# First routing of a mixture-of-experts layer: picks for all 32 tiles at once, expert starts added by TensorE, one-hots built tile by tile

## The chip, the cores and the metric

The kernel runs on one core of one Trainium2 chip. The metric is the device time of one execution in microseconds (us), as the median of several runs. The five engines are TensorE (PE; its weight loads are PEld), VectorE (DVE), ScalarE (ACT), GpSimd (POOL) and SyncE (SP), which issues most transfers.

## The reference

4096 rows of 128 values pass three layers, each with its own layer norm and a residual:

```python
x = x + 0.5 * ffn(layernorm(x))
x = x + attention(layernorm(x), context)
x = x + 0.5 * ffn(layernorm(x))

def ffn(x):                                   # 8 experts, 128 -> 512 -> 128
    gate_logits = einsum('bsd,ed->bse', x, gate_w) + gate_b + expert_bias
    top_idx = argmax(gate_logits, axis=-1)
    for e in range(8):
        mask = (top_idx == e)[..., None]
        h = relu(einsum('bsd,df->bsf', x, w1[e]) + b1[e])
        out = out + mask * (einsum('bsf,fd->bsd', h, w2[e]) + b2[e])
```

Only the expert with the largest logit serves a row. The attention has 8 heads of 128 and 512 keys from `context`; its scores are sharpened around their mean, and its bias `bout` is added at the end.

## The kernel before, in words

The 4096 rows lie in SBUF as 128 partitions x 32 tiles (`ROWS`, T = 32, two halves of HALF = 16 tiles, four chunks of CH = 8). A row is served by its expert in a sorted order: the rows of each expert fill whole tiles of 128 *slots*, at most SLOTS = 39 tiles. The kernel has three parts: the first expert layer with its routing and the preparation of the attention weights, the attention in 256 units with the second routing beside them, and the second expert layer. Each engine runs its own program, written out by hand; semaphores order them, and an engine that waits holds back everything behind it in its program.

The change is in the first 40 us, the first routing. In the order of the kernel's steps:

- `x_stats`, `x_moments` and `x_shift_of` (VectorE) and a power on GpSimd (L523) make the layer norm's scale and shift of each chunk. `x_transposes` and `x_gate` (TensorE) make the logits, half the tiles in bank 2, half in bank 3. `store_stats` (SP) writes each chunk's rows out to `x_stats` once its shift is there.
- `pick_rows(hf)` (VectorE, L899) turns the logits of one half into one-hots over the experts, `OHA`, in seven dependent steps, and sums them over the tiles (`SUMS`).
- `ranks0(hf)` (TensorE, L1441) counts for each row how many rows of the same expert stand before it: one matmul with `BEFORE`, 15 with `ONES`, and for the second half one for the sums of the first. `totals0` (L1457) counts the rows of each expert.
- `split_ranks(hf)` (VectorE, L927) picks the rank of the row's own expert and splits it into rank modulo 128 (`LOF`) and the rest (`HIF`). `places` (L984) works out from the totals how many tiles each expert has and where its slots start, picks that start for each row (L992, L994) and adds the rest of the rank over 128 (L995): the slot tile of each row, `SIDX`.
- `low_onehots(c)` (L945) compares a row of 0 to 127 with `LOF` of 8 tiles in one instruction, `slot_onehots(c)` (L998) a row of 0 to 38 with `SIDX`, and then multiplies by the row's number. `slot_rows(c)` (TensorE, L1466) multiplies the two, 8 matmuls a chunk, into bank 0. `rows_of_slots` (VectorE, L1007) makes from it the index `ISLOT`, by which GpSimd gathers the rows of each slot tile with indirect transfers (L536).
- Behind it on VectorE stand `experts_of_tiles`, `empty_slots` and eight `w1_low` (L1094).

Beside all this TensorE and ScalarE prepare the attention's products per head. `head_weights`, `head_transposes` and `head_products` (TensorE, L1603 to L1635) and the copies `ww_evac`, `wT_evac` and `keep` (ScalarE, L659 to L676) hand each other one head after the other; six of the eight heads stand before the expert layer. `keep_clock` (L1426) is a filler matmul whose result nobody reads. The order on TensorE is:

```python
            head_weights(0)
            head_transposes(1)
            ranks0(0)
            for _ in range(6):
                keep_clock(XT_BANK[0])
            ranks0(1)
            totals0()
            ...
            for h in range(BEFORE_FFN):      # head_rest(h); slot_rows(0) behind head 1,
                ...                          # (1) behind head 2, (2) and (3) behind head 3
```

Of the kernel before, what the change touches and what calls it, by code (L numbers as in the profile page):

```python
# [4 lines left out]
P = 128  # L5
# [3 lines left out]
def macaron_kernel(nc, x, context, Wq, Wk, Wv, Wout, bout, gate_w, gate_b, expert_bias, w1, b1, w2, b2, out):  # L9
# [13 lines left out]
    ALU = mybir.AluOpType  # L23
# [6 lines left out]
    T = N // P  # L30
# [31 lines left out]
    with ctx:  # L62
# [61 lines left out]
        with ExitStack() as prep:  # L124
# [6 lines left out]
            LG0 = sb("logits_first", [P, HALF, E], fp32, prep)  # L131
            MX0 = sb("row_max_first", [P, HALF], fp32, prep)
            RANK = sb("rank", [P, HALF], fp32, prep)
            RNI = sb("rank_int", [P, 2, HALF], i32, prep)
            LOF = sb("rank_low", [P, T], fp16, prep)
            HIF = sb("rank_high_rows", [P, T], fp32, prep)
            SWT = sb("start_by_tile", [P, T, E], fp32, prep)
            SIDF = sb("first_slot_of_row", [P, T], fp32, prep)
            SIDX = sb("slot_of_row", [P, T], fp16, prep)
            IOT = sb("iota_h", [P, P], fp16, prep)  # L140
            VALF = sb("row_number", [P, T], fp32, prep)
            VAL = sb("row_code", [P, T], fp16, prep)
# [69 lines left out]
        pick_step, picked, sums_ready = sem("pick_step"), sem("picked"), sem("sums_ready")  # L212
        rank0_ps, rank0_step, low_ready = sem("rank0_ps"), sem("rank0_step"), sem("onehot_low_ready")
# [64 lines left out]
        EMPTY_LINKS, EARLY_LINKS = 12, 13  # L278
# [576 lines left out]
        def _(dve):  # L855
# [43 lines left out]
            def pick_rows(hf):  # L899

                own = slice(HALF * hf, HALF * hf + HALF)
                wide = lambda b: b[:, :].unsqueeze(1).to_broadcast([P, HALF, E])
                over = lambda b: b.unsqueeze(2).to_broadcast([P, HALF, E])
                lg, chosen = LG0[:, :, :], OHA[:, own, :]
                logits = BK[LOGIT_BANK[hf]][:, LOGITS:LOGITS + HALF * E].rearrange("p (t e) -> p t e", e=E)
                done = 6 * hf
                dve.wait_ge(x_logits, NCH * (hf + 1))
                dve.wait_ge(x_rstd, 2 * (hf + 1))
                v.tensor_tensor(lg, logits, over(ROWS[:, own, RSTD]), ALU.mult).then_inc(pick_step, 1)
                dve.wait_ge(pick_step, done + 1)  # L910
                v.tensor_tensor(lg, lg, wide(GBEB), ALU.add).then_inc(pick_step, 1)
                dve.wait_ge(pick_step, done + 2)
                v.tensor_reduce(MX0[:, :], lg, AX.X, ALU.max).then_inc(pick_step, 1)
                dve.wait_ge(pick_step, done + 3)
                v.tensor_tensor(lg, lg, over(MX0[:, :]), ALU.is_ge).then_inc(pick_step, 1)
                dve.wait_ge(pick_step, done + 4)
                v.tensor_tensor(lg, lg, wide(PREF), ALU.mult).then_inc(pick_step, 1)
                dve.wait_ge(pick_step, done + 5)
                v.tensor_reduce(MX0[:, :], lg, AX.X, ALU.max).then_inc(pick_step, 1)
                dve.wait_ge(pick_step, done + 6)  # L920
                v.tensor_tensor(chosen, lg, over(MX0[:, :]), ALU.is_equal).then_inc(picked, 1)
                dve.wait_ge(picked, hf + 1)
                with nc.allow_low_precision(reason="whole numbers up to T are exact"):
                    v.tensor_reduce(SUMS[:, hf, :], chosen.rearrange("p t e -> p e t"), AX.X, ALU.add)\
                        .then_inc(sums_ready, 1)

            def split_ranks(hf):  # L927

                own = slice(HALF * hf, HALF * hf + HALF)
                done = 5 * hf  # L930
                dve.wait_ge(rank0_ps, hf + 1)
                counted = BK[LOGIT_BANK[hf]][:, RANKS0:RANKS0 + E * HALF].rearrange("p (t e) -> p t e", e=E)
                v.tensor_tensor(LG0[:, :, :], counted, OHA[:, own, :], ALU.mult).then_inc(rank0_step, 1)
                dve.wait_ge(rank0_step, done + 1)
                v.tensor_reduce(RANK[:, :], LG0[:, :, :], AX.X, ALU.add).then_inc(rank0_step, 1)
                dve.wait_ge(rank0_step, done + 2)
                v.tensor_copy(RNI[:, 0, :], RANK[:, :]).then_inc(rank0_step, 1)
                dve.wait_ge(rank0_step, done + 3)
                v.tensor_scalar(RNI[:, 1, :], RNI[:, 0, :], P - 1, None, ALU.bitwise_and).then_inc(rank0_step, 1)
                dve.wait_ge(rank0_step, done + 4)  # L940
                v.tensor_copy(LOF[:, own], RNI[:, 1, :]).then_inc(rank0_step, 1)
                dve.wait_ge(rank0_step, done + 5)
                v.tensor_tensor(HIF[:, own], RANK[:, :], LOF[:, own], ALU.subtract)
# [40 lines left out]
            def places():  # L984
# [806 lines left out]
```

## Time and profile before

| | us |
|---|---|
| median of 3 runs | 745.2 (745.04 to 745.28) |
| span of the profiled execution | 743.4 |
| TensorE busy | 711.0 (96%) |
| VectorE busy | 604.4 (81%) |
| ScalarE busy | 497.0 (67%) |
| GpSimd busy | 367.5 (49%) |

The span goes from the first instruction to the last; what lies around it is in the time of the runs and not in the span. Busy shares are means over three parts with different limits; for a change to one stretch they have to be read in that stretch.

### The profile page before, as it was taken

How to read it: one execution, taken by the hardware profiler on the slowest of the kernel's cores; microseconds unless marked ns; L12 is line 12 of the kernel's file. 1: busy time of each engine (PE TensorE's matmuls, PEld its weight loads, DVE VectorE, ACT ScalarE, POOL GpSimd, SP SyncE). 2: the span in 40 equal slices, each digit the busy share in tenths (PEclk: the TensorE clock that was granted, in tenths of full speed). 3: DMA queues.
4: the chain of work that ended last, by engine and by line, in shares of the span. 5: the costliest groups of instructions: out<-in, count | busy, mean ns of one | idle time of the engine just before them, and what ended most of it. 6: DMA issues, size and time to landing. Idle time of an engine off the chain costs nothing.

```text
span 743.4 us, 15250 instructions
## 1 busy us (share of the span) xinstructions
PE 711.0 (96%) x4374; PEld 595.6 (80%) x4374; DVE 604.4 (81%) x1645; ACT 497.0 (67%) x1212; POOL 367.5 (49%) x499
## 2 busy tenths in 40 slices
PE   9989999999999999999999999999999999989992
PEld 7768987788888788878878878887888887769991
DVE  6999999887787887878788788787878878688882
ACT  3687776677677677667667767766766666546661
POOL 5078886243343454345346335444534533486662
PEclk9999999999999999999999999999999999999996
DMA  9942432200000000000000000000000011232210
GB/s 252 342 148 49 96 90 61 63 16 1 2 0 1 2 11 5 2 4 12 0 1 15 2 1 12 5 0 4 13 1 1 16 44 70 89 86 64 59 47 5
DMA packets 31793, 31.49 MB, mean 42 GB/s; under 512 B 5050, under 2 KB 26184, under 8 KB 31201
## 3 DMA queue, kind: packets, MB, share of 16 engines
q1 hardware_dynamic: 27360, 23.91, 10.6%
q0 software_dynamic: 3520, 6.40, 3.4%
q8 instruction: 38, 0.62, 0.4%
q14 instruction: 43, 0.34, 0.2%
q10 hardware_dynamic: 832, 0.21, 0.1%
HBM read 20.96 MB, written 10.47 MB: 42 GB/s over the span
## 4 chain that ended last, share of the span: by engine, by line
PE 75%; DVE 15%; issue 3%; POOL 2%; DMA 1%; ACT 1%; DVEq 1%; another core or an unknown queue 0%; POOLq 0%; SPq 0%; ACTq 0%
PE bank L1478 16%; PE bank L1480 16%; PE bank L1479 16%; PE bank L1691 13%; PE bank L1527 5%; PE bank L1513 3%; DVE neg_max L1363 2%; DVE probsT_lo L1369 2%; PE bank L1530 2%; DVE hT_lo L1219 1%; DVE h L1198 1%; DMA rows<-in_L_attn_x 1%; PE bank L1537 1%; POOL rows L585 1%; DVE slot_rows L1202 1%
## 5 line engine op out<-in xcount | busy, mean ns | idle before, releaser
L601 POOL TENSOR_SCALAR probs<-probs,row_inv 128x512 f32<-128x512 f32 x256 | 178.4, 697 | 273.8 <-DVE row_inv L1374 263.0
L814 ACT ACTIVATE probs<-bank,neg_max 128x512 f32<-128x512 f32 x256 | 176.4, 689 | 144.0 <-DVE neg_max L1363 142.9
L1363 DVE TENSOR_REDUCE neg_max<-bank 128x1 f32<-128x512 f32 x256 | 176.4, 689 | 86.8 <-PE bank L1480 83.8
L1369 DVE TENSOR_TENSOR probsT_lo<-bank,probsT_hi 128x512 fp32r<-128x512 f32 x256 | 174.1, 680 | 2.2 <-ACT probsT_hi L823 2.0
L1691 PEld LDWEIGHTS bank<-ident,probs 128*128 128x128 f32 x1024 | 127.1, 140 | 38.6 <-POOL probs L601 2.6
L1691 PE MATMUL bank<-ident,probs 128*128 128x128 f32 x1024 | 153.5, 272 | 1.7 <-POOL probs L601 1.2
L823 ACT ACTIVATE probsT_hi<-bank 128x512 fp32r<-128x512 f32 x256 | 151.3, 591 | 2.1 <-PE bank L1691 2.1
L1478 PE MATMUL bank<-m_hi,xT_hi 128*128 128x512 f32 x256 | 122.4, 478 | 0.0
L1478 PE MATMUL bank<-probsT_hi,vw_hi 128*128 128x512 f32 x256 | 101.7, 397 | 3.6 <-DVE probsT_lo L1369 3.6
L1479 PE MATMUL bank<-probsT_lo,vw_hi 128*128 128x512 f32 x256 | 101.5, 396 | 0.0
L1480 PE MATMUL bank<-probsT_hi,vw_lo 128*128 128x512 f32 x256 | 101.4, 396 | 0.0
L1479 PE MATMUL bank<-m_lo,xT_hi 128*128 128x512 f32 x256 | 100.8, 394 | 0.0
L1480 PE MATMUL bank<-m_hi,xT_lo 128*128 128x512 f32 x256 | 100.6, 393 | 0.0
L1527 PE MATMUL bank<-w_hi_lo,hT_hi 128*128 x312 | 83.5, 344 | 7.3 <-DVE hT_lo L1219 5.6
L1530 PE MATMUL bank<-w_hi_lo,hT_lo 128*128 x312 | 69.6, 223 | 0.0
L1527 PEld LDWEIGHTS bank<-w_hi_lo,hT_hi 128*128 128x128 f32 x312 | 59.1, 190 | 12.2 <-issue 11.8
L766 ACT ACTIVATE hT_hi<-bank 128x512 fp32r<-128x512 f32 x78 | 46.7, 598 | 24.3 <-PE bank L1513 13.4
L1478 PEld LDWEIGHTS bank<-probsT_hi,vw_hi 128*128 128x128 f32 x256 | 48.0, 188 | 17.8 <-DVE probsT_lo L1369 6.8
L1198 DVE TENSOR_TENSOR h<-bank,b 128x512 f32<-128x512 f32 x78 | 53.5, 686 | 10.1 <-PE bank L1480 6.8
L1530 PEld LDWEIGHTS bank<-w_hi_lo,hT_lo 128*128 128x128 f32 x312 | 60.0, 192 | 0.0
L536 POOL DMA_INDIRECT slot_rows<-x_stats,row_of_slot x39 | 42.6, 1092 | 31.3 <-issue 28.7
L1480 PEld LDWEIGHTS bank<-m_hi,xT_lo 128*128 128x128 f32 x256 | 48.1, 188 | 11.2
(221 smaller groups left out, 1246.6 us busy)
## 6 DMA issues: line engine op xcount, KB each, us to landing
b<-in_L_ffn_b SPq DMA_DIRECT2D x4, 1024.0 KB, 6.3
x_packed<-slot_rows SPq DMA_DIRECT2D x39, 65.5 KB
slot_rows<-slots SPq DMA_DIRECT2D x39, 65.5 KB
x_stats<-rows SPq DMA_DIRECT2D x4, 524.0 KB, 10.2
rows<-x_packed SPq DMA_DIRECT2D x8, 262.0 KB, 2.6
rows<-in_L_attn_x SPq DMA_DIRECT2D x4, 512.0 KB, 8.2
w_lo<-in_L_ffn_w SPq DMA_DIRECT2D x8, 256.0 KB, 6.7
w_hi_lo<-in_L_ffn_w SPq DMA_DIRECT2D x8, 256.0 KB, 9.2
```

What stands on the lines that cost most here:

```text
L601: pool.tensor_scalar(PR[:, u % 4, :], PR[:, u % 4, :], RI[:, u % 4:u % 4 + 1], 1.0, ALU.mult, ALU.mult).then_inc(normed, 1)
L814: act.activation(PR[:, n % 4, :], BK[n % 2][:, :], ACT.Exp, bias=NM[:, n % 4:n % 4 + 1], accum_out=SU[:, n % 4:n % 4 + 1]).then_inc(probs, 1)
L823: act.activation(PTH[:, (u // G) % 2, :, (u % G) * P:(u % G + 1) * P], BK[2 + u % 2][:, :].rearrange("p (c q) -> p c q", c=KC), ACT.Copy)\
L1198: v.tensor_tensor(HB[:, j % 3, :].unsqueeze(1), BK[2 + j % 2][:, :].unsqueeze(1), B1[:, ds(e, 1), :], ALU.add).then_inc(s_hb, 1)
L1363: v.tensor_reduce(NM[:, n % 4:n % 4 + 1], BK[n % 2][:, :], AX.X, ALU.max, negate=True)\
L1369: v.tensor_tensor(PTL[at], BK[2 + u % 2][:, :].rearrange("p (c q) -> p c q", c=KC), PTH[at].bitcast(fp32), ALU.subtract).then_inc(pT_lo, 1)
L1478: pe.matmul(out_, wh, mh, start=start, stop=False)
L1479: pe.matmul(out_, wh, ml, start=False, stop=False)
L1480: return pe.matmul(out_, wl, mh, start=False, stop=stop)
L1527: pe.matmul(BK[6 + j % 2][:, 0:2 * D].rearrange("p (a s d) -> p a s d", a=1, s=2), HTH[:, j % 2, c * P:(c + 1) * P], W2HL[:, ds(e, 1), c, ...
L1530: last = pe.matmul(BK[6 + j % 2][:, 0:D].unsqueeze(1), HTL[:, j % 2, c * P:(c + 1) * P], W2HL[:, ds(e, 1), c, 0, :], start=False, stop=(c ...
L1691: last = pe.transpose(BK[2 + u % 2][:, c * P:(c + 1) * P], PR[:, u % 4, c * P:(c + 1) * P], IDN[:, :])
```

## The change

The picks run over all 32 tiles in one go: only the scaling of the logits, the last comparison and the sums are still two instructions, one for each half, and the shift of the last chunk stands between the two scalings. `ranks0` of both halves and `totals0` follow one another on TensorE, ahead of the six filler matmuls. VectorE works out the first slot of each expert (`first_slots`), in bf16, and TensorE adds it to every row's rank with one more matmul for each half (`add_starts`). `ONES` sums over the 128 partitions, so what is added is 128 times the expert's first slot tile, and what VectorE then picks is the row's place among all slots; one split gives its low part and its slot tile... in the same sum as the diff has it: one split gives the low part and the slot tile. The one-hots are built tile by tile, with the row's place as a scalar per partition; the comparison with the slot tile and the multiplication by the row's number become one instruction.

```diff
-            def pick_rows(hf):
+            def pick_rows():
...
+                for hf in range(2):
+                    own = slice(HALF * hf, HALF * hf + HALF)
...
+                    dve.wait_ge(x_logits, NCH * (hf + 1))
+                    dve.wait_ge(x_rstd, 2 * (hf + 1))
+                    v.tensor_tensor(LG0[:, own, :], logits, ROWS[:, own, RSTD].unsqueeze(2).to_broadcast([P, HALF, E]),
+                                    ALU.mult).then_inc(pick_step, 1)
+                    if hf == 0:
+                        x_shift_of(NCH - 1)
+                dve.wait_ge(pick_step, 2)
                 v.tensor_tensor(lg, lg, wide(GBEB), ALU.add).then_inc(pick_step, 1)
...
+                for hf in range(2):
+                    own = slice(HALF * hf, HALF * hf + HALF)
+                    v.tensor_tensor(OHA[:, own, :], LG0[:, own, :],
+                                    MX0[:, own].unsqueeze(2).to_broadcast([P, HALF, E]), ALU.is_equal)\
+                        .then_inc(picked, 1)
+                for hf in range(2):
+                    own = slice(HALF * hf, HALF * hf + HALF)
+                    dve.wait_ge(picked, hf + 1)
+                    with nc.allow_low_precision(reason="whole numbers up to T are exact"):
+                        v.tensor_reduce(SUMS[:, hf, :], OHA[:, own, :].rearrange("p t e -> p e t"), AX.X, ALU.add)\
+                            .then_inc(sums_ready, 1)
+
+            def places_of_rows():
+
+                for hf in range(2):
+                    own = slice(HALF * hf, HALF * hf + HALF)
+                    dve.wait_ge(rank0_ps, hf + 1)
+                    counted = BK[LOGIT_BANK[hf]][:, RANKS0:RANKS0 + E * HALF].rearrange("p (t e) -> p t e", e=E)
+                    v.tensor_tensor(LG0[:, own, :], counted, OHA[:, own, :], ALU.mult).then_inc(rank0_step, 1)
+                dve.wait_ge(rank0_step, 2)
                 v.tensor_reduce(RANK[:, :], LG0[:, :, :], AX.X, ALU.add).then_inc(rank0_step, 1)
...
+                dve.wait_ge(rank0_step, 6)
+                v.tensor_tensor(SIDX[:, :], RANK[:, :], LOF[:, :], ALU.subtract).then_inc(rank0_step, 1)
+                dve.wait_ge(rank0_step, 7)
+                v.tensor_scalar(SIDX[:, :], SIDX[:, :], 1.0 / P, None, ALU.mult).then_inc(rank0_step, 1)
 
             def low_onehots(c):
 
-                v.tensor_tensor(OHL[c], IOT[:, :].unsqueeze(1).to_broadcast([P, CH, P]),
-                                LOF[:, CH * c:CH * c + CH].unsqueeze(2).to_broadcast([P, CH, P]),
-                                ALU.is_equal).then_inc(low_ready, 1)
+                for i in range(CH):
+                    t = CH * c + i
+                    last = v.tensor_scalar(OHL[c][:, i, :], IOT[:, :], LOF[:, t:t + 1], None, ALU.is_equal)
+                last.then_inc(low_ready, 1)
...
-            def places():
+            def first_slots():
 
                 dve.wait_ge(total_ps, 1)
                 for i in range(3):
                     count_tiles(0, total0, P - 1, i, 1)
                 ends_of(0)
-                step, count = table_step[0], table_count[0]
-                link(v.tensor_tensor(starts, ends, tiles_of, ALU.subtract), step, count)
-                link(v.tensor_tensor(SWT[:, :, :], OHA[:, :, :], starts.unsqueeze(1).to_broadcast([P, T, E]), ALU.mult),
-                     step, count)
-                link(v.tensor_reduce(SIDF[:, :], SWT[:, :, :], AX.X, ALU.add), step, count)
-                link(v.scalar_tensor_tensor(out=SIDX[:, :], in0=HIF[:, :], scalar=1.0 / P, in1=SIDF[:, :],
-                                            op0=ALU.mult, op1=ALU.add), step, count)
+                v.tensor_tensor(STARTS[:, :], ends, tiles_of, ALU.subtract).then_inc(starts_ready, 1)
 
             def slot_onehots(c):
 
-                own = slice(CH * c, CH * c + CH)
-                over = lambda b: b[:, own].unsqueeze(2).to_broadcast([P, CH, SLOTS])
-                v.tensor_tensor(OHS[c], IOT[:, 0:SLOTS].unsqueeze(1).to_broadcast([P, CH, SLOTS]), over(SIDX),
-                                ALU.is_equal).then_inc(place_step, 1)
-                dve.wait_ge(place_step, c + 1)
-                v.tensor_tensor(OHS[c], OHS[c], over(VAL), ALU.mult).then_inc(place_ready, 1)
+                if c == 0:
+                    dve.wait_ge(rank0_step, 8)
+                for i in range(CH):
+                    t = CH * c + i
+                    last = v.tensor_scalar(OHS[c][:, i, :], IOT[:, 0:SLOTS], SIDX[:, t:t + 1], VAL[:, t:t + 1],
+                                           ALU.is_equal, ALU.mult)
+                last.then_inc(place_ready, 1)
...
-            pick_rows(0)
-            x_shift_of(NCH - 1)
-            pick_rows(1)
-            split_ranks(0)
-            split_ranks(1)
-            places()
+            pick_rows()
+            first_slots()
+            places_of_rows()
...
             def totals0():
 
                 pe.wait_ge(sums_ready, 2)
-                pe.wait_ge(rank0_step, 1)
...
+            def add_starts(hf):
+
+                pe.wait_ge(starts_ready, 1)
+                out_ = BK[LOGIT_BANK[hf]][:, RANKS0:RANKS0 + E * HALF].rearrange("p (t e) -> p t e", e=E)
+                pe.matmul(out_, ONES[:, :], STARTS[:, :].unsqueeze(1).to_broadcast([P, HALF, E]),
+                          start=False, stop=True).then_inc(rank0_ps, 1)
...
             head_transposes(1)
             ranks0(0)
+            ranks0(1)
+            totals0()
             for _ in range(6):
                 keep_clock(XT_BANK[0])
-            ranks0(1)
-            totals0()
+            add_starts(0)
+            add_starts(1)
             pe.wait_ge(ctxK_ready, 1)
             for h in range(BEFORE_FFN):
                 if h == 1:
-                    pe.wait_ge(rank0_step, 6)
+                    pe.wait_ge(rank0_step, 2)
                 head_rest(h)
```

## Rows read from the trace of the kernel before

**Rows 1.** Windows; busy us and count of each engine, clock, DMA share, GB/s

```profile
18.30:37.30 19.00, 17.36 (x167) 13.84 (x166) 17.24 (x51) 12.83 (x28) 0.00 (x0) 1.00 1.00 341
36.00:46.00 10.00, 9.48 (x61) 7.15 (x60) 9.67 (x24) 8.42 (x20) 7.08 (x6) 1.00 0.32 99
```

**Rows 2.** Chain of waits (start, us, what), 28 to 47 us

```profile
29.05 0.36 PE bank L1472 x8
```

**Rows 3.** Timeline of VectorE (start, us, line, out<-in, count, [idle before])

```profile
16.70 0.29 DVE L909 TENSOR_TENSOR logits_first<-bank,rows 128x128 f32<-128x128 f32 x1
...
21.28 0.29 DVE L921 TENSOR_TENSOR onehot_first<-logits_first,row_max_first 128x128 bf16<-128x128 f32 x1
21.61 0.38 DVE L924 TENSOR_REDUCE onehot_sums<-onehot_first 128x8 bf16<-128x128 bf16 x1
...
24.62 0.16 DVE L963 TENSOR_SCALAR counts_int<-bank 128x8 int32<-128x8 f32 x1
...
25.43 0.17 DVE L991 TENSOR_TENSOR counts<-counts 128x8 f32<-128x8 f32 x1
25.63 0.42 DVE L992 TENSOR_TENSOR start_by_tile<-onehot_first,counts 128x256 f32<-128x256 bf16 x1
26.09 0.42 DVE L994 TENSOR_REDUCE first_slot_of_row<-start_by_tile 128x32 f32<-128x256 f32 x1
...
26.77 1.22 DVE L947 TENSOR_TENSOR slot_rows<-iota_h,rank_low 128x1024 f16<-128x1024 f16 x1
...
34.56 0.48 DVE L1005 TENSOR_TENSOR xn_then_xnT_or_oT<-xn_then_xnT_or_oT,row_code 128x312 f16<-128x312 f16 x1
35.58 0.20 DVE L1013 TENSOR_SCALAR row_of_slot_f<-bank 128x39 f32<-128x39 f32 x1 [0.54 <-PE bank L1472]
```

**Rows 4.** Timeline of TensorE, 17 to 36 us

```profile
17.76 0.51 PE L1435 MATMUL bank<-gate_wT,xn_then_xnT_or_oT 128*128 128x8 f32 x4
...
19.98 0.22 PE L1446 MATMUL bank<-onehot_first,before 128*128 128x128 bf16 x1
...
20.55 0.82 PE L1427 MATMUL bank<-ones 128*128 128x256 bf16 x6
21.63 0.23 PE L1446 MATMUL bank<-onehot_first,before 128*128 128x128 bf16 x1 [0.27 <-DVE onehot_first L921]
...
22.33 0.19 PE L1462 MATMUL bank<-onehot_sums,ones 128*128 128x8 bf16 x2
22.46 1.10 PE L1623 MATMUL bank<-ctxT_sharp,wk_wqT_and_wv_wout 96*128 96x512 f32 x2
...
25.49 1.10 PE L1623 MATMUL bank<-ctxT_sharp,wk_wqT_and_wv_wout 96*128 96x512 f32 x2 [0.33 <-ACT wk_wqT_and_wv_wout L670]
...
29.05 0.36 PE L1472 MATMUL bank<-xn_then_xnT_or_oT,slot_rows 128*128 128x39 f16 x8 [0.86 <-DVE xn_then_xnT_or_oT L1005]
29.26 1.10 PE L1623 MATMUL bank<-ctxT_sharp,wk_wqT_and_wv_wout 96*128 96x512 f32 x2
...
34.77 0.36 PE L1472 MATMUL bank<-xn_then_xnT_or_oT,slot_rows 128*128 128x39 f16 x8
35.19 0.36 PE L1472 MATMUL bank<-xn_then_xnT_or_oT,onehot_low_rest 128*128 128x39 f16 x8
```

**Rows 5.** Timeline of GpSimd, at 16.5 us

```profile
16.51 1.65 POOL L523 TENSOR_TENSOR rows<-rows,nhalf 128x8 f32<-128x8 f32 x1 [1.05 <-DVE rows L873]
```

**Rows 6.** Timeline of VectorE, small or scalar operations at four places

```profile
3.44 0.27 DVE L889 TENSOR_SCALAR gate_w<-gate_w,gate_w_mean 8x128 f32<-8x128 f32 x1
...
6.84 0.64 DVE L869 BATCH_NORM_AGGREGATE rows<-bn_first 128x2 f32<-128x6 f32 x8
...
45.93 0.68 DVE L1111 TENSOR_SCALAR xn_then_xnT_or_oT<-xn_then_xnT_or_oT 128x1024 f32<-128x1024 f32 x1
...
130.16 0.59 DVE L1167 TENSOR_SCALAR xn_then_xnT_or_oT<-rows,rstd,shift 128x128 f32<-128x128 f32 x2
```

**Rows 7.** Timeline of ScalarE, at 28 us

```profile
28.01 0.37 ACT L670 ACTIVATE wk_wqT_and_wv_wout<-bank 96x256 f32<-96x256 f32 x1
```

More of the change, by code:

```diff
@@ L897, in gate_biases @@
                 dve.wait_ge(gw_step, 5)
-            def pick_rows(hf):
[L901 to L910, printed above, removed]
+            def pick_rows():
+                wide = lambda b: b[:, :].unsqueeze(1).to_broadcast([P, T, E])
+                over = lambda b: b[:, :].unsqueeze(2).to_broadcast([P, T, E])
+                lg = LG0[:, :, :]
+                for hf in range(2):
+                    own = slice(HALF * hf, HALF * hf + HALF)
+                    logits = BK[LOGIT_BANK[hf]][:, LOGITS:LOGITS + HALF * E].rearrange("p (t e) -> p t e", e=E)
+                    dve.wait_ge(x_logits, NCH * (hf + 1))
[5 more added lines that the diff above has]
+                dve.wait_ge(pick_step, 2)
@@ L911, in pick_rows @@
                 v.tensor_tensor(lg, lg, wide(GBEB), ALU.add).then_inc(pick_step, 1)
-                dve.wait_ge(pick_step, done + 2)
+                dve.wait_ge(pick_step, 3)
                 v.tensor_reduce(MX0[:, :], lg, AX.X, ALU.max).then_inc(pick_step, 1)
-                dve.wait_ge(pick_step, done + 3)
-                v.tensor_tensor(lg, lg, over(MX0[:, :]), ALU.is_ge).then_inc(pick_step, 1)
-                dve.wait_ge(pick_step, done + 4)
+                dve.wait_ge(pick_step, 4)
+                v.tensor_tensor(lg, lg, over(MX0), ALU.is_ge).then_inc(pick_step, 1)
@@ L917, in pick_rows @@
+                dve.wait_ge(pick_step, 5)
                 v.tensor_tensor(lg, lg, wide(PREF), ALU.mult).then_inc(pick_step, 1)
-                dve.wait_ge(pick_step, done + 5)
+                dve.wait_ge(pick_step, 6)
                 v.tensor_reduce(MX0[:, :], lg, AX.X, ALU.max).then_inc(pick_step, 1)
[L920 to L934, printed above, removed]
+                dve.wait_ge(pick_step, 7)
+                for hf in range(2):
[3 more added lines that the diff above has]
+                        .then_inc(picked, 1)
@@ L1446, in ranks0 @@
                 pe.matmul(out_, BEFORE[:, :], own, start=True, stop=False)
+                for i in range(HALF - 1):
+                    pe.matmul(out_[:, i + 1:HALF, :], ONES[:, :],
+                              own[:, i:i + 1, :].to_broadcast([P, HALF - 1 - i, E]), start=False, stop=False)
                 if hf:
@@ L1450, in ranks0 @@
                               start=False, stop=False)
-                for i in range(HALF - 1):
-                    last = pe.matmul(out_[:, i + 1:HALF, :], ONES[:, :],
-                                     own[:, i:i + 1, :].to_broadcast([P, HALF - 1 - i, E]),
-                                     start=False, stop=(i == HALF - 2))
-                last.then_inc(rank0_ps, 1)
             def totals0():
                 pe.wait_ge(sums_ready, 2)
-                pe.wait_ge(rank0_step, 1)
                 for hf in range(2):
```

35 lines of the change are left out of this document (16 added, 19 removed).

## The prediction

> **What bounds the kernel now.** I read the busy time by stretch first, then the chain of waits, then the three engines in order of time. In the first stage TensorE runs at its 2.4 GHz level without a break (PEclk 1.00), GpSimd does nothing from 18.3 to 37.3 us, and VectorE is busy 17.24 of 19.00 us, more than ScalarE and about as much as TensorE [rows 1]. So VectorE looks like the bound. The chain says that it stops being that at 29.05 us: there the chain passes to TensorE, at the first `slot_rows` [rows 2], and from there on it is the head products. What the change is worth is read from when each head starts, not from when VectorE has built its one-hots.
>
> VectorE now [rows 3]: picks from 16.70, starts of experts 24.62 to 25.6, first one-hot at 26.77, last one done at 34.56 + 0.48 = 35.04, `rows_of_slots` at 35.58 after a wait of 0.54 for TensorE. TensorE [rows 4]: `head_products(0)` at 22.46, head 1 at 25.49, a wait of 0.86 before `slot_rows(0)` at 29.05, head 2 at 29.26, `slot_rows(2)` and `(3)` at 34.77 and 35.19. `slot_rows(3)` takes 0.36, so `rows_of_slots` starts when it ends. These two waits, 0.86 and part of 0.42, are all that VectorE's one-hots cost today.
>
> **The change, step by step.** Durations come from one execution with a span of 743.4 us; the median of the runs is 745.2, so 1.8 us lie around the span, and I add the difference to either.
>
> *Picks.* All 32 tiles go through each step at once. A dependent step costs its duration plus 0.03 to 0.04 (L992 at 25.63 to L994 at 26.09 is 0.46 for 256 elements). Five steps, L911 to L919, become 5 x 0.46 in place of 10 x 0.33 (L921 at 21.28 to L924 at 21.61). But the scaling of the second half now stands ahead of all of them, and it waits for the logits of the last tile: their matmul ends at 17.76 + 0.51 = 18.27 [rows 4], and the last reciprocal root on GpSimd at 16.51 + 1.65 = 18.16 [rows 5]. So VectorE, which could go on at 17.0, stands until 18.30. Then: scaling 0.32, five steps 2.30, first `is_equal` at 20.92, done at 21.21; second at 21.13; sums at 21.33 and 21.63 (0.38 long, 0.08 of it overlapping), done at 22.01. Now the second `is_equal` starts at 21.28 and the first half's is done long before. The batching saves instructions, yet the last pick comes only 0.15 us sooner, and the first half's ranks start much later.
>
> *Ranks.* TensorE now does the first half's 16 matmuls from 19.98 to 20.55, beside VectorE's second picks. They move behind 21.21 + 0.06 = 21.27. Then 0.57 + 0.57, plus 0.05 for the sums' matmul, and the two totals, which start at 22.46 and end 0.19 later, at 22.65. Today they start at 22.33.
>
> *Starts.* `first_slots` begins at 22.70. L963 to L991 take 24.62 to 25.43 and 0.17 more, 0.98 in all, so `STARTS` is there at 23.68. Today these five links lie beside head 0; now TensorE waits for them in `add_starts(0)`, and everything queued behind it waits too: both head streams, and through them ScalarE. The six filler matmuls (0.82, modelled) cover part of that wait and cost nothing. The two new matmuls start at 23.74 and take about 0.055 each (16 narrower ones take 0.57), so `head_products(0)` starts at 23.85: **1.39 us later** than now. I keep 1.0 to 1.9 for that (below: all four handovers between the engines free and the ranks' matmuls running into each other; above: both halves at the 0.70 that 17 take from 21.63, and 0.1 for each handover).
>
> *Places and split.* They drop L992, L994 and L995 (25.63 to 26.77, 1.14). Two multiplications from 24.00 (0.53), one reduction of 256 (0.46) and five short links at 0.21 end the chain; the low one-hots may start at 25.94, 0.83 before today's 26.77.
>
> *One-hots tile by tile.* Twelve large instructions (0.51 x 8 and about 1.14 x 4; four chunks in 26.77 to 35.04, 2.07 each) become 64 small ones. No fp16 operation with a scalar per partition stands in the trace, so I bound it [rows 6]. A run of small instructions goes at 0.08 each (L869, 8 in 0.64, though a single one of that size, as L963, is 0.16 long), so most of the fixed part overlaps. L1111, with constants as scalars, handles 1024 elements in 0.68, so width costs little there; L889, with a scalar per partition, takes 0.27 for 128, or about 0.20 from start to start if 0.07 overlaps. Below: 0.08 + 0.08. Above: the two L1167 of 128 columns with two scalars take 0.59, at most 0.30 each, and 0.20 for the 39 columns (L1013 is that long), 0.50 a tile. I take 0.11 + 0.09 = 0.20, nearest to the fast rows, because GpSimd is idle here, as it is not in the stage of L1167. That is 1.6 a chunk and 25.94 + 6.4 = 32.3 for all, 2.7 before today.
>
> The Trainium skill, "VectorE: DVE Perf Modes", section on the perf-mode tiers, gives `tensor_scalar` on 16-bit data in SBUF four elements a cycle and `tensor_tensor` two. The trace differs on the second: L947, both inputs broadcast, takes 1.22 for 1024 fp16 elements, twice what that rule would make it. With the page's 58 cycles and four elements a cycle a low one-hot would be an estimated 0.09, and the sum would stay as it is.
>
> *What the heads make of it.* With the one-hots early, the pace is set by ScalarE's copies between the heads. Head 0 to head 1 is 3.03. Head 2 needs `ww_evac(2)`, done at 28.01 + 0.37 = 28.38 [rows 7], yet starts at 29.26 today: 0.84 of its start is the wait for one-hots. `slot_rows(0)` fits before it (free at 28.19, 0.21 long). So head 2 and 3 move by 1.39 - 0.84 = +0.55. At the fourth chunk there is 0.42 between `slot_rows(2)` and `(3)` where 0.21 would do: another 0.21 comes back. `place_ps`, heads 4 and 5 and the rest of the stage move by **1.39 - 1.05 = +0.34 us**. VectorE stands idle from 32.3 until then and gains nothing from its 2.7: the work behind, `rows_of_slots` and the eight `w1_low`, is queued behind that wait. From 36 to 46 us VectorE, TensorE and ScalarE are all full (9.67, 9.48, 8.42 of 10.00) [rows 1], so I let the shift through whole. `store_stats(3)` leaves about a microsecond earlier, but the DMA engines are full (share 1.00 to 37.3) and no wait in this stage ends on what follows it: nothing.
>
> Sum: span 743.4 + 0.34 = 743.7; median 745.2 + 0.35 = **745.6 us**. About 0.2% (1.5 us) is what a measurement can tell from no change, so this counts as no change.
>
> **Rivals.**
> (a) *The delay of head 0 is small and a little is won.* If it is under 1.05 (a later trace would show head 0 before 23.5), the sign turns; it can't win more than 1.05, the two waits, so 744.2 to 745.2. For it: all times above lean on handovers of 0.06. Against: STARTS needs ten dependent instructions behind 18.3. This never leaves 0.2%.
> (b) *The 64 small one-hots are slow: the other side.* Place: the fourth chunk. `slot_rows(3)` is due at 35.53 now, so a tile may cost (35.4 - 25.94)/32 = 0.29 before it decides. At L889's rate (0.20, and 0.12 for 39 columns) the chunk ends at 36.2 and the span grows by 1.1: 746.3, still within 0.2%. If each instruction pays its whole duration, 0.39 to 0.50 a tile, the end is at 38.4 to 41.9, +3.3 to +6.8: 748.5 to 752.0. For it: L1167. Against: L869, L1111 [rows 6]. The same page says that the next VectorE operation waits until the pipeline has drained, and advises 512 elements and more a tile; the back-to-back L869 rows speak against the whole cost.
> (c) *TensorE's clock falls.* It idles now from 20.2 to 21.27 and again near 23.4; today it has filler there. If it drops to 1.2 GHz ahead of head 0, each head's roughly 2.5 us of matmul (22.46 to 24.9) becomes 5, over its pace of 3.03, so 2 us a head: 747.5 for one, 749.5 for two. For it: those idle pieces. Against: 1.00 throughout, also across the 0.86 at 28.2 [rows 1, 4]. The skill, "TensorE: Matmul & The Clock Gate", Part 1, says that the clock halves after idling; no row here shows that in this stage.
> (d) *Unchanged otherwise, but later stages fall differently* (gathers, weight loads, the shared ports): a few tenths either way.
>
> **Chances.** Forecast (head 0 late by 1.05 to 1.9, one-hots in time) 0.66; (a) 0.16; (b) mild 0.06, (b) full 0.05; (c) 0.04; the rest 0.03, faster by more than 0.2%. Same = 0.66 + 0.16 + mild (b) 0.06 less 0.03 for sums of small losses = 0.85; slower = 0.05 + 0.04 + 0.03 = 0.12; faster 0.03. The range, 744.3 to 747.2, takes in (a), the mild (b) with its +1.1 on a delay at the upper bound, and some tenths of (d); it leaves out the full (b) and (c).
>
> **What would show it.** Right: second scaling at 18.3; `add_starts(0)` at 23.7 with TensorE idle before it; head 0 at 23.8 to 23.9; no wait of TensorE at `slot_rows(0)`; a wait of some 3 us of VectorE ahead of `rows_of_slots`, which starts at 35.9. Wrong: head 0 before 23.5; a tile's pair of one-hots over 0.29; PEclk below 1.00 between 20 and 30 us; or a shift at 50 us that isn't the shift at 36.

## The result, and the profile after

Measured side by side, the changed kernel takes 750.07 us (median of 9 runs, 747.04 to 753.02), the kernel before 745.24 (9 runs, 744.19 to 746.79): ratio 1.0057, 95% interval 1.0041 to 1.0072. The forecast of 745.6 in a range of 744.3 to 747.2 was wrong; the change makes the kernel slower, by 4.8 us between the medians (3.1 to 5.4 by the interval). The profiled execution has a span of 749.3, 5.9 over that of before. Medians and ratios here and below leave out executions more than 1.5% above their kernel's fastest, which occurred only in the three kernels with tiles innermost (three to five of twelve, at 757 to 764 us).

VectorE in order of time, after the change (columns as in [rows 3]):

```profile
18.24 0.17 DVE L875 SCALAR_TENSOR_TENSOR rows<-rows 128x8 f32<-128x8 f32 x1 [1.20 <-POOL rows L522]
...
20.94 0.49 DVE L925 TENSOR_TENSOR onehot_first<-logits_first,row_max_first 128x128 bf16<-128x128 f32 x2
...
22.70 0.17 DVE L974 TENSOR_SCALAR counts_int<-bank 128x8 int32<-128x8 f32 x1 [0.69 <-PE bank L1462]
...
25.96 1.39 DVE L959 TENSOR_SCALAR slot_rows<-iota_h,place_low 128x128 f16<-128x128 f16 x8
27.26 1.69 DVE L1009 TENSOR_SCALAR xn_then_xnT_or_oT<-iota_h,slot_of_row,row_code 128x39 f16<-128x39 f16 x8
...
35.96 1.70 DVE L1009 TENSOR_SCALAR xn_then_xnT_or_oT<-iota_h,slot_of_row,row_code 128x39 f16<-128x39 f16 x8
38.20 0.20 DVE L1019 TENSOR_SCALAR row_of_slot_f<-bank 128x39 f32<-128x39 f32 x1 [0.54 <-PE bank L1479]
```

Up to 25.96 this is the forecast almost to the hundredth: the last shift at 18.24 and the second scaling behind it, first `is_equal` at 20.94 (20.92 forecast), `first_slots` at 22.70, the first one-hot at 25.96 (25.94). The step that fails comes next. Eight low one-hots take 1.30 (25.96 to 27.26) and eight slot one-hots, of 39 columns only, take 1.60: 2.90 a chunk, 0.363 a tile. 0.20 was forecast, and 0.29 was worked out as the price from which VectorE holds up `slot_rows(3)`. The last one ends at 35.96 + 1.70 = 37.66, 2.6 later than before, and `rows_of_slots` starts at 38.20, where it was at 35.58 [rows 3].

TensorE, the answer to [rows 4]:

```profile
23.75 0.29 PE L1470 MATMUL bank<-first_slot_of_expert,ones 128*128 128x128 bf16 x2 [0.41 <-DVE first_slot_of_expert L1001]
23.88 1.07 PE L1630 MATMUL bank<-ctxT_sharp,wk_wqT_and_wv_wout 96*128 96x512 f32 x2
...
29.43 0.36 PE L1479 MATMUL bank<-xn_then_xnT_or_oT,slot_rows 128*128 128x39 f16 x8
...
35.37 0.36 PE L1479 MATMUL bank<-xn_then_xnT_or_oT,slot_rows 128*128 128x39 f16 x8
37.80 0.36 PE L1479 MATMUL bank<-xn_then_xnT_or_oT,onehot_low_rest 128*128 128x39 f16 x8 [2.07 <-DVE xn_then_xnT_or_oT L1009]
38.01 1.98 PE L1630 MATMUL bank<-ctxT_sharp,wk_wqT_and_wv_wout 96*128 96x512 f32 x2
...
43.01 2.06 PE L1630 MATMUL bank<-ctxT_sharp,wk_wqT_and_wv_wout 96*128 96x512 f32 x2
...
46.52 0.82 PE L1430 MATMUL bank<-ones 128*128 128x256 bf16 x6
```

`add_starts` at 23.75 and head 0 at 23.88, 1.42 later than before (1.39 forecast). Heads 0 to 3 go on without waiting for one-hots, as forecast. Then TensorE stands for 2.07 us ahead of `slot_rows(3)`. And behind it the same two matmuls of L1630 that took 1.07 in head 0 take 1.98: the clock has fallen. Its rows, by stretch (columns as in [rows 1]; the clock is the third number from the end):

```profile
24.00:36.00 12.00, 11.32 (x93) 8.93 (x92) 11.78 (x65) 8.64 (x20) 0.00 (x0) 1.00 1.04 372
36.00:38.00 2.00, 0.20 (x8) 0.23 (x9) 1.66 (x9) 0.56 (x2) 0.00 (x0) 1.00 0.48 143
38.00:46.00 8.00, 8.00 (x36) 5.71 (x33) 6.94 (x17) 3.12 (x6) 5.08 (x4) 0.57 0.29 90
```

TensorE is busy for 0.20 of the 2 us from 36 to 38. PEclk is 1.00 there and 0.57 in the mean of 38 to 46: the lower of the two levels, 1.2 GHz, nearly all the way to 45. The six fillers behind head 5 start 8.72 after `slot_rows(3)` (46.52 - 37.80). In the kernel before it is 5.72 (40.91 - 35.19). The chain of waits names the same two causes one after the other: eight slot one-hots (from 36.05), `slot_rows(3)` (37.80), two slow matmuls of L1630 (from 38.16). The fillers before, and the first addition of `b1` in the expert layer before and after:

```profile
40.91 0.82 PE L1427 MATMUL bank<-ones 128*128 128x256 bf16 x6
...
47.43 0.69 DVE L1198 TENSOR_TENSOR h<-bank,b 128x512 f32<-128x512 f32 x1 [0.82 <-issue]
```

```profile
53.03 0.69 DVE L1201 TENSOR_TENSOR h<-bank,b 128x512 f32<-128x512 f32 x1 [0.82 <-DVE xn_then_xnT_or_oT L1117]
```

So of the 5.9 us of this execution about 2.6 come from VectorE being late and 3.0 from TensorE's clock: 46.52 - 40.91 = 5.61, of which 37.80 - 35.19 = 2.61 stand already at `slot_rows(3)`. At `b1` the shift is still 5.6.

### The profile page after: what moved, and what is told of

Its sections match the earlier page's. It is cut to its first block, busy times and chain, and to the rows that moved or that the text cites. A ratio compares the mean times of both kernels' runs of the same rounds, so it can differ in the third digit from the quotient of the medians.

```text
span 749.3 us, 15293 instructions
## 1 busy us (share of the span) xinstructions
PE 714.4 (95%) x4376; PEld 597.9 (80%) x4376; DVE 604.6 (81%) x1685; ACT 496.3 (66%) x1212; POOL 367.4 (49%) x499
## 4 chain that ended last, share of the span: by engine, by line
PE 79%; DVE 13%; POOL 2%; issue 2%; DMA 1%; ACT 1%; another core or an unknown queue 0%; POOLq 0%; DVEq 0%; SPq 0%; ACTq 0%
PE bank L1485 16%; PE bank L1487 16%; PE bank L1486 16%; PE bank L1700 13%; PE bank L1534 6%; PE bank L1520 4%; DVE neg_max L1366 2%; DVE probsT_lo L1372 2%; PE bank L1537 2%; PE bank L1544 1%; DMA rows<-in_L_attn_x 1%; POOL rows L584 1%; DVE xn_then_xnT_or_oT L1009 1%; PE bank L1741 1%; DVE h L1201 1%
```

## Experiments

The short diffs are against the kernel that each text names. The times of one group of runs were taken on one chip beside the same runs of the kernel before.

**All one-hots large again.**

```diff
             def low_onehots(c):
...
-                for i in range(CH):
-                    t = CH * c + i
-                    last = v.tensor_scalar(OHL[c][:, i, :], IOT[:, :], LOF[:, t:t + 1], None, ALU.is_equal)
-                last.then_inc(low_ready, 1)
+                v.tensor_tensor(OHL[c], IOT[:, :].unsqueeze(1).to_broadcast([P, CH, P]),
+                                LOF[:, CH * c:CH * c + CH].unsqueeze(2).to_broadcast([P, CH, P]),
+                                ALU.is_equal).then_inc(low_ready, 1)
...              slot_onehots: is_equal, then mult by VAL, over 8 tiles at once, as in the kernel before
```

> The changed kernel with the one-hots of the kernel before: three large instructions a chunk in place of 16 small ones; picks, ranks, added starts and split stay as changed. Theory A (the tile-by-tile one-hots, 0.36 us a tile, hold TensorE at slot_rows(3), and that idle stretch brings its clock down): one-hots end at 25.96 + 4 x 2.07 = 34.2, slot_rows(3) at about 35.5, rows_of_slots at 35.9, no wait over 0.5 us and PEclk 1.00 between 20 and 50 us; time 745.6, +0.3 to +0.4 on the kernel before. Theory B (the later picks and TensorE's waits at 20.2 and 23.4 are what costs, and what brings the clock down): the clock still falls and the time stays near 749 to 750.

Measured: 743.92 against 744.33 us, ratio 0.9995 (0.9976 to 1.0014). VectorE in order of time, and the clock from 38 to 46:

```profile
25.90 1.22 DVE L957 TENSOR_TENSOR slot_rows<-iota_h,place_low 128x1024 f16<-128x1024 f16 x1
...
33.69 0.48 DVE L1011 TENSOR_TENSOR xn_then_xnT_or_oT<-xn_then_xnT_or_oT,row_code 128x312 f16<-128x312 f16 x1
35.91 0.20 DVE L1019 TENSOR_SCALAR row_of_slot_f<-bank 128x39 f32<-128x39 f32 x1 [1.74 <-PE bank L1479]
```

```profile
38.00:46.00 8.00, 7.48 (x49) 5.58 (x48) 7.85 (x16) 7.24 (x19) 6.47 (x6) 1.00 0.34 102
```

First one-hot at 25.90, last ended at 34.17, `rows_of_slots` at 35.91: 0.33 after that of before [rows 3], where the forecast had 0.34. It waits 1.74 for TensorE, which stays at 1.00. The picks, the ranks, the added starts, TensorE's wait for them and its idling of 1.14 us ahead of 21.2 are all still in this kernel, and so are places kept in fp32: the changed kernel makes `LOF`, `SIDX` and `VAL` fp32 in place of fp16, which the diff of the change does not show. Theory B falls: they cost about what was forecast, and they don't bring the clock down. The whole loss goes with the form of the one-hots.

**Fillers where TensorE waits.**

```diff
                 if h == 3:
                     slot_rows(2)
+                    pe.wait_ge(head_kept, 6)
+                    for _ in range(20):
+                        keep_clock(VW_BANK[2])
                     slot_rows(3)
```

The wait ahead of the fillers is for the bank that they write to.

> The changed kernel with 20 filler matmuls of 0.107 us each between slot_rows(2) and slot_rows(3), where TensorE waits 2.07 us for VectorE. Theory A: slot_rows(3) still at 37.8, but PEclk 1.00 behind it, so the heads after it run at the old pace; the span is 2.6 us over the kernel before, 747.8 us, and the runs lie closer together than 747.0 to 753.0. Rival (the clock falls for what happens ahead of 35 us, or the later part of the loss has another cause): the clock still falls near 38 us and the time stays at 750.

Measured: 745.91 against 744.33, ratio 1.0024 (1.0003 to 1.0045). TensorE in order of time:

```profile
35.51 2.34 PE L1430 MATMUL bank<-ones 128*128 128x256 bf16 x20
37.74 0.36 PE L1479 MATMUL bank<-xn_then_xnT_or_oT,onehot_low_rest 128*128 128x39 f16 x8
37.95 1.10 PE L1630 MATMUL bank<-ctxT_sharp,wk_wqT_and_wv_wout 96*128 96x512 f32 x2
...
40.90 1.12 PE L1630 MATMUL bank<-ctxT_sharp,wk_wqT_and_wv_wout 96*128 96x512 f32 x2 [0.24 <-ACT wk_wqT_and_wv_wout L669]
```

`slot_rows(3)` is as late as in the changed kernel (37.74), but the head behind it takes 1.10 for its two large matmuls and not 1.98, and the next starts 2.95 later and not 5.00 (38.01 to 43.01 there). The first addition of `b1` is at 50.2, 2.8 over before, in place of 53.0. The clock's part is shown to be a part of its own, about 3 us in a profiled execution, and to hang on this idle stretch. The 2.6 that remain lie inside the interval (0.2 to 3.3 us). One expectation failed: the twelve runs spread over 6.2 us (744.56 to 750.79), no less than those of the changed kernel, so the spread has another source; the profiled execution took 750.09 and loses another 2 us somewhere behind `b1` (span 748.2, 4.8 over before); the cause of that stays open.

**Only the one-hots of the change, in the kernel before.**

```diff
-            LOF = sb("rank_low", [P, T], fp16, prep)      # SIDX and VAL likewise
+            LOF = sb("rank_low", [P, T], fp32, prep)
...              low_onehots and slot_onehots tile by tile, as in the change
```

> The kernel before with only its one-hots made tile by tile (and their places kept in fp32); picks, ranks and places as before. Theory A: one-hots from 26.8 at 2.9 us a chunk, the last at 38.4, slot_rows(3) at 38.5, 3.4 us later than before, with TensorE idle for over 3 us ahead of it and the clock down behind it: 748.5 without and about 752 with the clock's part. Theory B (the order of the picks and the added starts costs): near 745.

Measured: 748.56 against 744.33, ratio 1.0055 (1.0034 to 1.0076): about the loss of the whole change, from this one part. TensorE in order of time:

```profile
29.96 0.36 PE L1472 MATMUL bank<-xn_then_xnT_or_oT,slot_rows 128*128 128x39 f16 x8 [1.73 <-DVE xn_then_xnT_or_oT L1003]
...
38.67 0.36 PE L1472 MATMUL bank<-xn_then_xnT_or_oT,onehot_low_rest 128*128 128x39 f16 x8 [2.54 <-DVE xn_then_xnT_or_oT L1003]
38.87 1.85 PE L1623 MATMUL bank<-ctxT_sharp,wk_wqT_and_wv_wout 96*128 96x512 f32 x2
```

Now it waits twice, 1.73 at the first chunk too, since the heads start early here; `slot_rows(3)` is at 38.67 (38.5 expected), and the 1.85 behind it is the low clock again. The idle stretch ahead of it is 2.54 and not over 3, because `slot_rows(2)` comes late too. The median is 4.2 over before, between the 3.4 expected without the clock's part and the nearly 7 with it; the profiled execution, with it, took 752.65 and was the longest of ten. So most executions seem to lose less to the clock than the one profiled.

**The price of one small instruction.** The series stand behind `rows_of_slots` and write to a tile that nobody reads any more, so they change nothing but the time of the stage.

```diff
+                price(0, P, 3.0, None, None)        # 128 columns, constant
+                price(1, P, one, None, None)        # one scalar per partition
+                price(2, P, one, 2.0, ALU.mult)
+                price(3, P, one, two, ALU.mult)     # two
+                ...                                 # the same with 39 and with 8 columns
```

> The changed kernel with eleven series of eight small VectorE comparisons added behind rows_of_slots, written to a tile that is no longer read: fp16, 128, 39 or 8 columns, with no, one or two scalars per partition. The stage gets about 12 us longer, so only the distances within a series count. If the width sets the price: 39 columns cheaper than 128 in every form. If each scalar per partition has its own price: about 0.08 to 0.11 us from start to start with constants, 0.16 with one, 0.20 with two, whatever the width.

From its one execution (758.33 us); eight instructions a row, columns start, us, line, operation, names, shapes:

```profile
39.13 0.91 DVE L1030 TENSOR_SCALAR onehot_low_rest<-iota_h 128x128 f16<-128x128 f16 x8
40.07 1.46 DVE L1030 TENSOR_SCALAR onehot_low_rest<-iota_h,slot_of_row 128x128 f16<-128x128 f16 x8
...
42.99 1.94 DVE L1029 TENSOR_SCALAR onehot_low_rest<-iota_h,slot_of_row,row_code 128x128 f16<-128x128 f16 x8
44.97 0.73 DVE L1030 TENSOR_SCALAR onehot_low_rest<-iota_h 128x39 f16<-128x39 f16 x8
...
46.51 1.22 DVE L1030 TENSOR_SCALAR onehot_low_rest<-iota_h,slot_of_row 128x39 f16<-128x39 f16 x8
47.77 1.70 DVE L1029 TENSOR_SCALAR onehot_low_rest<-iota_h,slot_of_row,row_code 128x39 f16<-128x39 f16 x8
49.50 1.21 DVE L1030 TENSOR_SCALAR onehot_low_rest<-iota_h,slot_of_row 128x8 f16<-128x8 f16 x8
50.74 1.63 DVE L1029 TENSOR_SCALAR onehot_low_rest<-iota_h,slot_of_row,row_code 128x8 f16<-128x8 f16 x8
52.41 0.67 DVE L1029 TENSOR_SCALAR onehot_low_rest<-iota_h 128x8 f16<-128x8 f16 x8
```

From the start of a series to that of the next, over eight: with 128 columns 0.118 with a constant (39.13 to 40.07), 0.186 with one scalar per partition, and 0.25 with two (42.99 to 44.97). With 39 columns 0.096 with constants (44.97 to the next series, at 45.74), 0.158 with one, 0.216 with two. With 8 columns 0.155 with one and 0.209 with two. A series ends with a wait, which puts a few hundredths on each. So a scalar per partition (fp32 here) costs about 0.06 us for each instruction, two cost about 0.12, whatever the width, while the step from 8 to 128 columns costs 0.03 to 0.04. That is why the 39-column slot one-hot, with two, is dearer (0.20) than the 128-column low one, with one (0.163). The fused comparison and product saved nothing: in the large form both together are 0.91 for 8 tiles, in the small one 1.60.

**One half at a time**, against the changed kernel: only the slot one-hots large (the first text), only the low ones large (the second).

```diff
+ first:   slot_onehots(c) with two large tensor_tensor;  low_onehots(c) stays tile by tile
+ second:  low_onehots(c) with one large tensor_tensor;   slot_onehots(c) stays tile by tile
```

> The changed kernel with only the slot one-hots large again (two instructions a chunk), the low ones tile by tile. A chunk: 8 x 0.163 + 0.91 = 2.2, so the last ends at 25.96 + 8.85 = 34.8, ahead of the 35.4 at which TensorE comes to slot_rows(3). If the heads' pace is the threshold: no wait of TensorE, PEclk 1.00, rows_of_slots at 35.9, time as with all one-hots large.

> The changed kernel with only the low one-hots large again, the slot ones tile by tile with two scalars each. A chunk: 1.14 + 1.60 = 2.74, the last ends at 36.9, slot_rows(3) at 37.1, 1.6 late, TensorE idle for 1.4: rows_of_slots at 37.5, 1.9 over the kernel before. If 1.4 us of idling are enough for the clock to fall, up to 3 more; if not, PEclk stays 1.00 and about 747 to 747.5.

Measured on one chip: 745.42 and 747.04, against 745.64 before; ratios 0.9994 (0.9979 to 1.0010) and 1.0023 (1.0006 to 1.0040). The last chunk on TensorE in the first and in the second, and the second's clock from 38 to 46:

```profile
35.67 0.36 PE L1480 MATMUL bank<-xn_then_xnT_or_oT,onehot_low_rest 128*128 128x39 f16 x8
```

```profile
37.21 0.36 PE L1478 MATMUL bank<-xn_then_xnT_or_oT,onehot_low_rest 128*128 128x39 f16 x8 [1.41 <-DVE xn_then_xnT_or_oT L1008]
```

```profile
38.00:46.00 8.00, 7.48 (x52) 5.77 (x51) 7.82 (x18) 6.48 (x15) 5.37 (x5) 1.00 0.29 92
```

With 0.276 a tile TensorE doesn't wait, with 0.342 it waits 1.41: the threshold of 0.29 lies between. And with 1.41 us of idling ahead of `slot_rows(3)` the clock stayed at its 2.4 GHz level (1.00), where it fell after 2.07, 2.08 and 2.54. The two halves don't add up: the small low one-hots alone lose nothing, the small slot ones alone, which looked like the saving, 1.4 us (0.4 to 3.0), and both together 4.6 in this group, because only then is the clock's part in it.

**The changed kernel once more**, unedited, in the same group.

> The changed kernel once more, on the same chip as the three beside it, for the size of its loss on the same runs of before. Expected 4 to 6 us over the kernel before where the clock falls behind slot_rows(3), some 2.5 where it doesn't.

Measured: 750.23 (6 runs) against 745.64, ratio 1.0064 (1.0042 to 1.0087). Three stretches of it, and TensorE around the second idle stretch, here and in the first profile:

```profile
38.00:42.00 4.00, 4.00 (x20) 3.14 (x17) 3.67 (x12) 1.20 (x2) 1.76 (x2) 0.57 0.05 13
42.00:46.00 4.00, 3.70 (x27) 2.71 (x25) 3.28 (x6) 3.27 (x8) 3.39 (x3) 1.00 0.54 163
...
56.00:58.00 2.00, 2.00 (x11) 1.83 (x10) 2.00 (x5) 0.60 (x1) 0.88 (x1) 0.50 0.04 12
```

```profile
54.46 0.33 PE L1544 MATMUL bank<-ident,slot_xn 128*128 128x128 f32 x1 [1.47 <-ACT slot_xn L748]
...
55.61 1.12 PE L1520 MATMUL bank<-ident,h 128*128 128x128 f32 x4
```

```profile
56.01 0.33 PE L1544 MATMUL bank<-ident,slot_xn 128*128 128x128 f32 x1 [1.58 <-ACT slot_xn L748]
...
57.16 0.66 PE L1520 MATMUL bank<-ident,h 128*128 128x128 f32 x4
```

The idling ahead of `slot_rows(3)` is the same to a hundredth (2.08), but the clock is back by 42 us, where it took until 45 in the first profile. And it falls a second time at about 55.5, behind a wait of 1.47 us for ScalarE (the next transposes take 1.12); in the first profile the same wait is 1.58 and the clock stays (0.66). The kernel with only the small one-hots falls there too, after 1.40, and stayed at 1.00 after its 1.73 at `slot_rows(0)`. So the length of an idle stretch does not decide by itself: after 1.40 and 1.47 the clock fell, after 1.41, 1.58 and 1.73 it did not. The first addition of `b1` is at 51.6 here and at 53.0 there. How much the clock takes differs from one execution to the next. The six runs have mean clocks of 0.982 to 0.986 against a median of 0.990 in the runs of before, and among the nine first shown the clock goes from 0.985 (753.0 us) to 0.992 (747.2); but the 29 runs of before in this group spread as widely (743.28 to 748.30), so the spread alone says little.

**Tiles innermost.** An idea for cheaper one-hots, against the kernel before: the large instructions, but with a stored iota of 128 x 8 and every operand read with step 1 in its innermost dimension. TensorE then reads each tile with a step of 8.

```diff
+                v.tensor_tensor(OHL[c], IOT[:, :, :],
+                                LOF[:, CH * c:CH * c + CH].unsqueeze(1).to_broadcast([P, P, CH]), ALU.is_equal)
...
-                    last = pe.matmul(BK[PLACE_BANK][:, 0:SLOTS], OHL[c][:, i, :], OHS[c][:, i, :],
+                    last = pe.matmul(BK[PLACE_BANK][:, 0:SLOTS], OHL[c][:, :, i], OHS[c][:, :, i],
```

> The kernel before with its large one-hot instructions, but the tiles innermost in them: a stored iota of 128 x 8, the places of 8 tiles read with step 1, fp16 throughout. If VectorE's rate of one element a cycle in L947 came from the broadcast innermost dimension, 1024 elements now take about 0.6 us in place of 1.22 and a chunk 1.2 in place of 2.07, so the one-hots end at 31.6; TensorE no longer waits at slot_rows(0), and rows_of_slots starts about 1.0 earlier, at 34.5: time 1 us under the kernel before at the most, since the heads set the pace (the prediction's 1.05). If the rate doesn't change: the same time as before.

Measured: 746.13 against 745.85, ratio 1.0021 (0.9997 to 1.0044). VectorE, then TensorE, then GpSimd and TensorE at the start of the kernel:

```profile
27.59 0.69 DVE L947 TENSOR_TENSOR slot_rows<-iota_h,rank_low 128x1024 f16<-128x1024 f16 x1
...
36.72 0.20 DVE L1012 TENSOR_SCALAR row_of_slot_f<-bank 128x39 f32<-128x39 f32 x1 [4.28 <-PE bank L1471]
```

```profile
35.29 0.79 PE L1471 MATMUL bank<-xn_then_xnT_or_oT,slot_rows 128*128 128x39 f16 x8
35.89 0.80 PE L1471 MATMUL bank<-xn_then_xnT_or_oT,onehot_low_rest 128*128 128x39 f16 x8
```

```profile
2.66 1.92 POOL L504 IOTA iota_h<- 128x1024 f16 x1
...
4.80 0.24 PE L1582 MATMUL bank<-ident,gate_w 8*128 8x8 f32 x1 [1.06 <-POOL row_number L506]
```

VectorE did what was expected: 0.69 for the 1024 in place of 1.22, 1.19 a chunk in place of 2.07. TensorE took it back: eight matmuls of `slot_rows` take 0.60 from start to start (35.29 to 35.89) in place of 0.21, four times over. The gain was expected to be small and became none. Its head 0 also starts at 23.47, 1.0 late, and that comes from the edit as well: the stored iota, eight times as large, takes GpSimd 1.92 us in place of 0.23, TensorE waits 1.06 for GpSimd at 4.80, the eight fillers behind that take 1.89 in place of 1.09, ScalarE's copies come late, and VectorE waits 0.72 for one of them at 17.41. (In the last of the three kernels with this iota the same fillers took 1.05 and head 0 is at 22.36, so the wait alone does not do it.) Without the late start the stage would be about as long as before (an estimate: the first addition of `b1` is at 48.53, 1.1 over before).

On top of it, the last two chunks earlier on TensorE; and, in the second text, the added starts inside head 0 as well (their diff stands with the last experiment):

```diff
                 if h == 2:
                     slot_rows(1)
-                if h == 3:
                     slot_rows(2)
                     slot_rows(3)
```

> As the kernel with tiles innermost, and slot_rows(2) and (3) behind head 2 on TensorE in place of behind head 3. If TensorE's order is what holds the gathers once the one-hots are early: rows_of_slots starts near 32.1 in place of 34.5, and the row gathers and the eight w1_low with it; the heads keep their times. The experts' first tiles then wait for the heads and for ScalarE only: 1 to 3 us under the kernel before. Rival (heads and ScalarE already set the end of the stage): no more than the 1 us of the run without the early order.

> As the kernel with early slot_rows, and in addition the changed kernel's added starts, with picks half by half as before and add_starts placed behind the first matmul of head 0, so that TensorE doesn't stand: head 0 within 0.1 of 22.5, one-hots from 25.8 in place of 26.8. Expected 0 to 0.5 us under the run without them, because the heads set the pace: the added starts alone are worth little.

Both missed: 747.53 and 747.54 against 745.85, ratios 1.0034 (1.0003 to 1.0064) and 1.0031 (1.0011 to 1.0051). `rows_of_slots` did come at 34.21 and 33.56 in place of 36.72, but head 5 starts at 39.89 and 39.23, later than the 38.34 of before: the slow `slot_rows` take 0.6 each in place of 0.2 and now all stand ahead of it, and the first of the two kernels has the late start as well. VectorE then waits 2.78 us for ScalarE at its first expert tile in either, and the first addition of `b1` comes at 50.03 and 48.65, no earlier than the 48.53 without the early order. The heads and ScalarE set the end of this stage, not the gathers: the rival that the first text names.

**The added starts without TensorE's wait.** Against the changed kernel: picks half by half as before, large one-hots with places in fp16, the six fillers between the two `ranks0` again, and `add_starts` between the two products of head 0. The last of these in the diff:

```diff
                 pe.matmul(BK[M_BANK[h]][:, :], WW[:, 0, :], CTXK[:, :], start=True, stop=True).then_inc(m_ps, 1)
+                if h == 0:
+                    add_starts(0)
+                    add_starts(1)
```

> The changed kernel's added starts and single split alone, with the large one-hots and the picks half by half of the kernel before, and add_starts behind the first matmul of head 0. Theory: head 0 at 22.5 (1.4 earlier than in the changed kernel), one-hots from 25.8 to 34.1, slot_rows(3) at 34.2, rows_of_slots at 34.6: 1.0 us under the kernel before, PEclk 1.00. Rival (the places are not worth anything because something behind 36 us sets the end): equal to the kernel before.

> The version with added starts inside head 0, picks half by half and large one-hots, once more: rows_of_slots at 34.8, 0.8 before that of the kernel before; expected 0 to 1 us under the kernel before and 4 to 6 under the changed one.

Measured: 744.86 against 745.85, ratio 0.9992 (0.9971 to 1.0014), and 744.57 against 745.64, ratio 0.9986 (0.9969 to 1.0003). VectorE, then TensorE, in the first of the two:

```profile
25.65 1.22 DVE L948 TENSOR_TENSOR slot_rows<-iota_h,place_low 128x1024 f16<-128x1024 f16 x1
...
34.81 0.20 DVE L1010 TENSOR_SCALAR row_of_slot_f<-bank 128x39 f32<-128x39 f32 x1 [0.89 <-PE bank L1472]
```

```profile
34.41 0.36 PE L1472 MATMUL bank<-xn_then_xnT_or_oT,onehot_low_rest 128*128 128x39 f16 x8
```

Head 0 is at 22.22, the one-hots begin at 25.65, `rows_of_slots` at 34.81, 0.77 before that of the kernel before. In the second trace these are 22.30, 25.73 and 34.89. In its traces the version is better where it should be, and it clearly beats the changed kernel (744.57 against 750.23 in one group). Against the kernel before the medians are 1.0 us lower both times, but neither interval leaves 1 out. It is likely the better one, not shown to be.

## Why the prediction was wrong, step by step

*Picks, ranks, starts, places:* right. 25.96 for 25.94, head 0 at 23.88 for 23.85. The last hundredths are luck: by its own terms the chain ends at 26.04 (24.00 + 0.53 + 0.46 + five links of 0.21), and the fifth link took only 0.09. With the one-hots restored their net cost was +0.33 at `rows_of_slots`, for +0.34.

*One-hots tile by tile:* wrong, and this is the failed step. "I take 0.11 + 0.09 = 0.20, nearest to the fast rows": it is 0.163 + 0.200 = 0.363. Its own sign of being wrong, a pair over 0.29, came true. The run of small instructions that the prediction leaned on, L869 at 0.08 each [rows 6], reads no scalar per partition; each such scalar costs 0.06, and a comparison with constants takes 0.10 to 0.12. L889, with one, was in the rows and gave 0.20 for 128 columns, above the 0.163 measured. I set it aside for the low one-hots and priced the slot ones by their 39 columns, where columns hardly cost anything. The upper bound of 0.50 held and the value was taken from the wrong end. The reason given, that GpSimd is idle, did not make it so: GpSimd is idle from 24 to 36 us after the change as well (0.00 of 12.00).

*What the heads make of it:* the mechanism and its threshold were right, 0.29 a tile, bracketed by the runs at 0.276 and 0.342. Rival (b) had the right place. At its "mild" price of 0.32 it gave +1.1; at 0.363 its own formula gives 25.94 + 11.6 = 37.6 and +2.5 (2.61 measured). That alone is 747.7 and outside the range.

*Rival (c), the clock:* looked for in the wrong place. It was weighed for the idling at 20 to 23 us, where nothing happened, alone and not behind (b). But (b) produces the idle stretch that (c) needs: behind TensorE's wait of 2.07 us the lower clock cost about 3 us more. Its price of 2 us a head was right: the next head starts 5.00 after the slowed one, for 2.95. The two were given 0.05 and 0.04 as if apart, and their sum, which is what was measured, stood nowhere. The Trainium skill, "TensorE: Matmul & The Clock Gate", Part 1, says that idling halves the clock; the trace now agrees, 1.00 to 0.50 and the same matmuls at 1.98 for 1.07.

*The skill on small instructions:* "VectorE: DVE Perf Modes", section on the DRAIN, has the next operation wait for the pipeline, and one that is not held start earlier. With constants the runs show 0.10 to 0.12 for each, less than one takes alone (0.17), so not the whole cost is paid; the direction of the page's advice, wide instructions, was right here. Its tier table, which gives 16-bit two-input operations twice the rate, came true once every operand was read with step 1 (0.69 for 1.22), and not with a broadcast innermost dimension. So the difference that the prediction found in L947 belongs to that form of operand.

## What to carry to other kernels

Price a small instruction by its operands, not by its width: find a row with the same kinds of operands, and where there is none, let the nearest one with a scalar per partition count for more than a faster row without. When a rival creates a wait of TensorE, multiply it out with the clock's rival; they are not two events. And when an engine's work is cheapened by a layout, look at who reads it, and at who has to write it.

## What the runs showed of the hardware that was not expected

- A scalar per partition (fp32) costs VectorE about 0.06 us an instruction, from 8 to 128 columns alike (0.155 with one and 0.209 with two at 8 columns). No run has fp16 ones, so whether they cost the same stays open.
- TensorE's matmuls with operands at a step of 8 fp16 elements: 0.075 each in place of 0.026, for 39 columns.
- After 2.07 and 2.08 us of idling TensorE's clock fell from 1.00 to 0.50 and stayed low until 45 in one execution and 42 in another of the same kernel; after 2.54 it fell too. Of the shorter idle stretches two were followed by a fall (1.40 and 1.47) and three were not (1.41, 1.58, 1.73). What else decides stays open.
